# Two heads' row maxima beside two heads' scores in one ring of four PSUM pairs, and other seams between the stages

## The reference, cut

```python
# causal attention: x is (2, 512, 256), 16 query heads, 4 key heads, 16 features a head
q, k = _rope(q, N_EMBD), _rope(k, N_EMBD)
k, v = jnp.repeat(k, 4, axis=1), jnp.repeat(v, 4, axis=1)
att = jnp.einsum('bhqd,bhkd->bhqk', q, k) / scale
att = jax.nn.softmax(jnp.where(causal[None, None], att, -jnp.inf), axis=-1)
y = jnp.einsum('bhqt,bhtd->bhqd', att, v)
out = y.transpose(0, 2, 1, 3).reshape(b, t, n) @ Wo.T + bo

# both ffn kinds: 8 experts of 176, 2 per token, and a shared part (704 wide in L0, 176 in L1)
probs = jax.nn.softmax(x @ gate_w.T, axis=-1)
w, chosen = jax.lax.top_k(probs, 2)
for e in range(8):
    w_e = jnp.where(chosen == e, w, 0.0).sum(-1)
    out = out + w_e[:, None] * (silu_and_mul(x @ w13[e].T) @ w2[e].T)
out = out + shared            # silu_and_mul(x @ gate_up.T) @ down.T
```

## Time and profile before

| | us |
|---|---|
| median of three runs | 1767.59 (1763.21 to 1771.33) |
| profiled execution | 1765.34 |
| its span | 1763.6 |

### The profile page before, as it was taken

One profiled execution on the slowest core, in us unless ns is written; L12 is line 12 of the kernel. 1 busy time (PEld: TensorE's weight loads), 2 busy tenths in 40 slices (PEclk: granted clock), 3 DMA queues, 4 the chain that ended last, 5 costly groups with the idle time before them and its releaser, 6 DMA issues. The chain is left out here.

```text
span 1763.6 us, 28160 instructions
## 1 busy us (share of the span) xinstructions
PE 1507.1 (85%) x10208; PEld 1138.0 (65%) x10208; DVE 913.2 (52%) x1981; ACT 748.1 (42%) x1863; POOL 409.2 (23%) x328
## 2 busy tenths in 40 slices
PE   6999999984998689999999799968887895899787
PEld 4777788873876557677676587744445674633665
DVE  5766666663624446565555562464444414366622
ACT  5665746550343243433434334323333342477142
POOL 2507070400253320111101025310000361100063
PEclk9999999996899799999999989977887797899699
DMA  3001020102522201010100062210001423000423
GB/s 146 25 33 59 1 91 2 54 2 60 195 72 90 93 13 31 0 42 0 42 0 1 5 222 66 96 44 1 1 1 48 158 93 100 1 1 1 166 83 127
DMA packets 42741, 99.90 MB, mean 57 GB/s; under 512 B 7168, under 2 KB 21760, under 8 KB 42240
## 3 DMA queue, kind: packets, MB, share of 16 engines
q1 hardware_dynamic: 32480, 69.85, 11.4%
q0 software_dynamic: 9984, 28.32, 4.8%
q10 hardware_dynamic: 160, 0.13, 0.0%
HBM read 79.93 MB, written 18.35 MB: 56 GB/s over the span
## 5 line engine op out<-in xcount | busy, mean ns | idle before, releaser
L780 DVE TENSOR_TENSOR s_h_e<-s_bank,s_silu_e 128x176 f32<-128x176 f32 x92 | 31.4, 341 | 188.7 <-ACT s_silu_e L586 188.7
L465 PE MATMUL s_bank<-s_expert_w,s_xe 128*128 x368 | 127.5, 470 | 0.8 <-ACT s_xe L580 0.7
L124 POOL TENSOR_SCALAR ln_var<-ln_moments 128x4 f32<-128x4 f32 x16 | 4.1, 254 | 532.6 <-DVE ln_moments L117 450.4
L338 POOL DMA_INDIRECT s_xg<-normed_rows,s_from_row x92 | 91.0, 989 | 135.6 <-DVE s_from_row L709 108.8
L345 POOL DMA_INDIRECT expert_rows<-s_y,s_to_row x92 | 91.1, 990 | 93.6 <-ACT s_y L598 76.5
L2451 POOL TENSOR_TENSOR s_w_hi<-s_w_raw,zero 128x1024 fp32r<-128x1024 f32 x25 | 55.3, 2214 | 218.1 <-PE s_memory L80 188.0
L1106 ACT ACTIVATE s_scratch<-s_bank,s_neg_max 128x128 f32<-128x128 f32 (+3 forms) x128 | 67.2, 527 | 89.0 <-DVE s_neg_max L1187 89.0
L489 PE MATMUL s_bank<-s_expert_w,s_he 88*128 x368 | 95.4, 381 | 4.9 <-ACT s_he L592 4.9
L1187 DVE TENSOR_REDUCE s_neg_max<-s_bank 128x1 f32<-128x128 f32 (+3 forms) x128 | 59.7, 487 | 74.2 <-PE s_bank L1015 74.1
L78 PE MATMUL s_bank<-xn_t_hi,s_w_hi 128*128 128x512 f32 x208 | 93.0, 447 | 4.8 <-DVE s_w_lo L1160 3.0
L1032 PE MATMUL s_bank<-s_probs_t,s_v 128*128 128x512 f32 (+3 forms) x256 | 76.2, 441 | 20.7 <-ACT s_probs_t L1114 20.7
(11 more groups left out here) (374 smaller groups left out, 4349.5 us busy)
## 6 DMA issues: line engine op xcount, KB each, us to landing
s_expert_w<-in_experts SPq DMA_DIRECT2D x32, 608.0 KB, 12.7
s_w_raw<-in_wa_o SPq DMA_DIRECT2D x16, 512.0 KB, 3.8
s_yg<-expert_rows SPq DMA_DIRECT2D x32, 256.0 KB, 4.3
s_raw<-in_shared SPq DMA_DIRECT2D x16, 384.0 KB, 7.0
normed_rows<-s_ln_xn POOLq DMA_DIRECT2D x8, 512.0 KB, 9.4
s_w_raw<-in_wa_k SPq DMA_DIRECT2D x4, 512.0 KB, 4.0
s_w_raw<-in_wa_v SPq DMA_DIRECT2D x4, 512.0 KB, 3.5
s_w_raw<-in_wa_q SPq DMA_DIRECT2D x4, 512.0 KB, 4.9
```

The costliest lines, as they stand in the source:

```text
L338: pool.indirect_dma_start(out=xg[:, i % XG_RING, :], out_offset=None, in_=x_rows[:, :], in_offset=bass.IndirectOffsetOnAxis(ap=from_row[:, ...
L465: last = pe.matmul(u_bank[i % 2][:, 0:2 * INTER], xe[:, i % 2, x], expert_of(P, i, w), start=c == 0, stop=c == DC - 1, skip_group_check=True)
```

## The change

- `Norm` and `measure`: an ffn stage measures only tiles 0 to 3 for the next one and issues no root. The attention stage behind it measures tiles 4 to 7 itself and issues both roots.
- ffn: the logits are formed with the gate weights held and 512 tokens moving, 12 matmuls into two banks; ScalarE copies them to SBUF (`logits_t`), and PE turns them back with eight matmuls of 16 columns. ScalarE's `high(1)` and `high(2)` come behind the two copies.
- ffn with two shared pieces (L1): `up(1, .)`, its `h_of` and `h_low` come behind the tiles, piece 0's `h_of` and `h_low` behind `from_row`; at the end the tiles are added first, then the shared part.
- wide: wq is loaded behind wk in two halves by columns, and split half by half; the second half of the norm's high and low parts comes behind the split of wk; PE's fills of Q wait for their half alone.
- root mean square: the wait for `loaded` comes behind fill 2.
- causal: one ring of four PSUM pairs holds everything; `step(U, x)` forms two heads' maxima of unit U+1 beside the other two heads' scores of unit U; each j has its own exponentials, and the four attends follow the eight steps.

```diff
     def gpsimd(self, pool):
-        if not self.measured:
-            self.of.root(pool, 0)
-        self.of.root(pool, 1, ready=self.measured)
+        if self.measured != "both":
+            self.of.root(pool, 0, ready=self.measured == "first")
+        self.of.root(pool, 1, ready=self.measured == "both")
...
-            if out is None:
-                following.root(pool, 0)
...
+                at = slice(half * HALF, (half + 1) * HALF)
+                for c in range(DC):
+                    last = product(pe, logit_bank[half][:], (gate_hi[:, c, :], gate_lo[:, c, :]),
+                                   (res.xh[:, c, at], res.xl[:, c, at]), c == 0, c == DC - 1)
+                last.then_inc(logits_ready, 1)
+            for half in range(NHALF):
+                pe.wait_ge(logits_copied, half + 1)
                 for t in range(half * TB, (half + 1) * TB):
...
+                    last = pe.matmul(token_bank[:, t * 16:(t + 1) * 16], logits_t[:, t * P:(t + 1) * P], res.ident[:, 0:16],
+                                     start=True, stop=True, skip_group_check=True)
...
-            up(1, 0)
-            up(1, 1)
+            if early:
+                up(1, 0)
+                up(1, 1)
             list_rows()
...
-            load(0)
-            for c in range(DC):
-                sp.dma_start(wq_raw[:, c, :], t["wb_q"][:, c, :]).then_inc(wq_loaded, 16)
...
+            load(0, load_queries)
...
-            pe.wait_ge(loaded, 16 * 6)
             pe.wait_ge(ones_made, 1)
             for m in range(FILLS):
                 fill(m)
+                if m == 2:
+                    pe.wait_ge(loaded, 16 * 6)
...
+                for x in range(PAIR_STEPS):
+                    j, p = divmod(x, 2)
+                    if ahead:
+                        order.append(("natural", U + 1, TB - 1 - j, p))
+                    order.append(("scores", U, j, 1 - p))
+                    if x == 1:
+                        order += [("turn", U - 1)] * (U > 0) + [("q", U + 2)] * (U + 2 < UNITS)
+                    if x == 3:
+                        order += [("back", U - 1)] * (U > 0)
+                    if x == 5 and not ahead:
+                        order += [("out", n) for n in outs_in(U)]
+                order.append(("att", U))
+                if ahead:
+                    order.append(("shift", U + 1))
+                    order += [("out", n) for n in outs_in(U)]
...
-                if place[step] >= 3:
-                    pe.wait_ge(*read(ring[place[step] - 3]))
+                if place[step] >= RING:
+                    pe.wait_ge(*read(ring[place[step] - RING]))
```

VectorE's and ScalarE's lists in the causal stage follow the new order:

```diff
             for U in range(UNITS):
-                exponentials(U, 0, 0)
-                exponentials(U, 0, 1)
                 if U:
                     copy_o(U - 1)
-                if U + 2 < UNITS:
-                    high_q(U + 2)
...
+                for j in range(TB):
+                    exponentials(U, j, 1)
+                    exponentials(U, j, 0)
+                    if j == 0 and U + 2 < UNITS:
+                        high_q(U + 2)
+                    if j == 1 and U:
+                        high_o(U - 1)
                 if U + 1 < UNITS:
                     shifted(U + 1)
```

418 lines of the change are left out of this document (228 added, 190 removed).

## The result

The changed kernel takes 1699.32 us (median of four runs, 1697.57 to 1700.07), the kernel before 1766.88 in the four runs beside it; the ratio is 0.9615 with a 95% interval of 0.9591 to 0.9639.

What follows compares the result with a forecast made beforehand. The order of work, no engine, was taken to bound the causal loop, with idle seams second. Terms of -51.9 us from the profiled 1765.3 gave 1713.4, or 1715.7 with the median's 2.3 added; range 1700 to 1742.

Steps and rivals of the forecast that it cites:

- the clock's: Causal loop: fewer stops of PE raise its mean clock from 0.80 to 0.85, -8 us, bounds 0 to -13.
- Seams: Three seams behind ffn stages: VectorE's idle time follows POOL's power and falls to 1.05 us each, -9.2 us in all.
- Rival B: Seams: the wait comes with POOL's indirect transfers, not its power, and stays; +9.2, 1725 us; about 0.1 in or near the forecast.
- Wide start: Wide stage's start: earlier wq in halves removes PE's wait, -6.1, and the earlier K split gives -1.1; -7.2 us taken.
- ffn starts: ffn stages' start: wide logits and shared work moved back save 5.2 us in each L1 stage, 1.0 in each L0.
- The row against the rule: ffn logits: trace's 0.213 us per 16-column matmul taken over the skill's 60-cycle overhead, by which wide logits cost 5 us a stage.
- ffn end of L1: End of ffn stages with two shared parts: later shared work adds 1.5 us in stage 5 and 2.8 in the last.
- stage 6's start: Root-mean-square stage: +1.75 us for statistics, -2.6 for the first fill no longer waiting on a load; -0.9 us.
- Causal loop: Causal stage's loop: maxima beside other heads' scores cut idle time by 18 us and a higher clock gives 8; -26 us.
- A: Causal loop: steps move the waiting, clock stays at 0.80, gain 0 to 10 us, total 1732 to 1742; chance 0.17.
- C: Causal loop: idle time falls but the clock doesn't rise, 1724 us; about 0.1 in or near the forecast.
- D: Causal loop: frequent short stops keep PE's clock at half throughout, total 1808 us; chance 0.04.

Runs made afterwards that it cites:

- the run with the loads behind: The changed kernel with wk, wv and wo loaded ahead of wq again, wq still in halves by columns: 1734.88 us, 0.9582 of the kernel before.
- The run with `low_o` earlier: The changed kernel with VectorE's low_o ahead of the maxima of row tile 1 of the first pair in the causal loop: 1722.95 us, 0.9525 of the kernel before.
- causal alone: The kernel before with the changed causal stage alone: 1732.82 us, 0.9794 of the kernel before.
- narrow logits: The changed kernel with the 48 logits matmuls of 16 columns put back in all four ffn stages: 1744.33 us, 0.9623 of the kernel before.

## Why the prediction was right and where it was wrong

**The step that failed** is the clock's. The sum gave the loop 8 us for it (0.80 to 0.85) and every other stage nothing, without a reason. The runs showed 20.3 us less busy time in the loop at 0.89, and 6.2 us less in stage 6 at 0.92 instead of 0.88. An idle term that came out 5.4 us too large hid part of this, so that the total missed the range by only 0.7 us. Why the clock of stage 6 rose stays open.

**Seams.** Right in size: 9.2 us forecast, and 3.1, 3.1 and 2.5 us seen at the three. The reason given, POOL's power, was too narrow: a power and an addition behind the indirect transfers do it alike. Rival B fell, since the transfers alone leave 1.2 us.

**Wide start.** -7.2 forecast. Stages 1 and 2 together gave -11.35 against -11.5 for all terms in them. The working moved the loads and halved them and put most of the gain down to the order; the run with the loads behind shows that halves alone do it. Between the two stages 2 us lie on the other side of the border: stage 1's end didn't come as early as the sum said. Its tiles end 0.6 us earlier, but the clock was lower behind them, and PE clears its accumulators 1.0 us later within the stage than before.

**ffn starts.** The L1 stages: -2.45 and then -5.4 in the rows, against -2.5 and -5.2. Part of that agreement is luck: in the changed kernel the first logits matmul came 5.77 us after the start instead of 4.91, and the wide ones ran at 0.74 instead of the half clock that the working took. In other runs of the same code VectorE read stage 5's logits 10.9 to 13.8 us after the start. The L0 stages gave 0.85 us at the logits and 0.6 at `from_row`, against 1.0. Not priced was that a wait for `earlier` came out from under the narrow matmuls; on the path it cost little, if anything. The row against the rule was the right choice: the price of a small matmul comes from the trace.

**ffn end of L1, stage 6's start.** Stage 5 -6.1 against -6.4. Stage 6's first fill started 6.5 us after the stage's start instead of 8.0, where the working had a gain of 0.8; of the 7.5 us that the stage lost, 6.2 are PE's busy time.

**Causal loop.** The sum took 18 us of idle and 8 of clock ("from 0.80 to 0.85"); the loop gave 12.6 of idle and 20.3 of busy time, at 0.89. The idle part was too large because `low_o` had been placed behind a row maximum, a hand-over that the prediction's list of what is late next left out; it named step 0 and attend 0. The run with `low_o` earlier gave 5.4 us of idle time back. The clock part was too small for two reasons. The clock rose to 0.89, beyond the 0.88 behind the upper bound of 13. And the formula is too weak: it gives 140.9 x (1-0.80/0.89) = 14.2 at 0.89, where 20.3 came. It takes busy time times mean clock as fixed, and that product fell from 112.7 to 107.3; a mean over a stretch also counts the clock of its idle time. The Trainium skill, "TensorE: Matmul & The Clock Gate", section on PSUM-queue depth-cycling, was cited for the case that the 8 us stay away. The loop still cycles through its pairs and still has both levels (units at 0.81 and at 1.00), as the page has it; that the mean can't rise does not follow from it, and at 0.89 it did rise.

**Clock outside the loop.** Stages 6 and 7 gave 6.6 and 2.2 us more than forecast. In stage 6 nearly all of it is busy time of unchanged matmuls; in stage 7 PE is busy 7.0 us less, 4.5 of it over the logits, and idle 2.4 more. The sum treated the clock of a stage as its own property. Stage 6 through all runs shows that it isn't: one code had 0.89 to 0.94. A few us on either side for stages like these belong into a range; two of them at 5 us would have put its lower end near 1690.

**Rivals.** A (the steps move the waiting) fell for four pairs; with three, at 221 us, it came out worse than A had it. B fell as worded, see the seams. C (no gain in clock) and D (half clock throughout) fell at 0.89.

## What to carry to other kernels

Where PE stops for a microsecond or two every few, price such a stop at more than its length: in the one pair that shows it, 5.5 us of removed waits were worth 9.2. Don't read a few us in one stage of one profile as the effect of an edit in that stage; one code of stage 6 took 161.3 to 167.7 us here. Compare busy time, idle time and granted clock, and look at the same stage in several kernels, on one chip, before you name a cause. When one of two engines' work is laid beside the other's, look at the number of buffers between them (three pairs against four were 48 us here), and then for a release that is still queued behind something that nobody waits for.

## What the runs showed of the hardware that I had not expected

- POOL, behind indirect transfers and then one arithmetic instruction of 0.20 us, took 5.23 us until its first instruction behind the seam; behind arithmetic without indirect transfers in the stage it took 1.12 us, and with transfers alone the seam was 1.2 us.
- One stage of 864 matmuls, unchanged, took between 161.3 and 167.7 us in eleven runs, at a mean clock of 0.94 to 0.89. Two of them began 0.04 us apart, at 1461.65 and 1461.69, and differed by 3.3 us.
- Over the logits, 48 matmuls of 16 columns each with weights of their own, the granted clock was 0.50 to 0.74 in the twelve stages that have them (the kernel before, causal alone, narrow logits), although PE was busy throughout. Over the wide form it was 0.69 to 1.00 in all runs.
- VectorE's scaling of 16 columns, 0.17 us in the kernel before, took 2.37 us in the changed kernel while POOL was in a subtraction, which itself took 4.52 us instead of 2.39:

```profile
592.34 2.37 DVE L1198 TENSOR_SCALAR s_bq<-s_bq 128x16 f32<-128x16 f32 x1
...
590.16 4.52 POOL L955 TENSOR_TENSOR s_w_lo<-s_w_raw,s_w_hi 128x1024 fp32r<-128x1024 f32 x1
...
596.60 2.39 POOL L955 TENSOR_TENSOR s_w_lo<-s_w_raw,s_w_hi 128x1024 fp32r<-128x1024 f32 x1
```

VectorE's subtraction of wq's second half (2.29 us from 590.13) and POOL's lie over one another there, and VectorE's 16 columns end with POOL's subtraction, at 594.7. By the Trainium skill ("GPSIMD Engine Reference", section Specifications) the two share their interfaces to SBUF and contend when VectorE's instruction has two inputs there; POOL's 4.52 us beside such a subtraction agree. Why the 16 columns with one input waited too isn't shown.
